# Transposes of the batch norm and the middle attention stage moved to DMAs per subtile, and SyncE's issues reordered

## The chip, the cores and the metric

The kernel runs on one core of a Trainium2 chip. The metric is the device time of one execution in microseconds (us), median of the runs shown; lower is better. Engines: PE is TensorE (matmuls), ACT is ScalarE, DVE is VectorE, POOL is GpSimd, SP is SyncE, whose queue (SPq in the profile) issues most DMAs.

## What is computed

Four graph layers over 10,000 nodes with 512 features and 5,000 edges, each followed by a residual and a layer norm. The change touches the tail of layer 1 (GraphSAGE with batch norm) and the start and middle of layer 2 (two graph attention convolutions):

```python
# layer 1, tail
h = (h - mu) * rsqrt(var + EPS) * gamma + beta
x = layernorm(x + relu(h) + x)
# layer 2, gat_conv twice; x:[n,d_in], W:[d_in,H*C], H = 4, C = 256
h = (x @ W).reshape(n, H, C)
...
out = segment_sum(h[src] * alpha[:, :, None], dst) + bias
x1 = relu(gat_conv(x, W1)); x2 = relu(gat_conv(x1, W2)); x2 @ Wfc + bfc
```

## The kernel before, in words

The program is a row of stages; at the end of each, all five engines meet at one semaphore. Nodes are padded to G = 20 groups of 512, each group being S = 4 subtiles of 128 rows. Every f32 matmul is made of three f16 ones (`split_product`, lines 324 to 326): an operand is split in a high half and the low half that is left, and lo x hi, hi x lo and hi x hi are summed in a PSUM bank. The stationary operand of a product has to have the features on the partitions, so rows (nodes on the partitions) have to be transposed first.

**`batch_norm_stage(kn, "sage")`** (lines 2037 to 2275) loads for group g the batch-norm input `b_h` (features on the partitions) and the residual rows `b_x`. ACT applies scale, shift and Relu (`apply`, L2186, 4 instructions a group). PE transposes the result to rows (`turn_rows`, L2230, 16 matmuls of 128x128 against an identity a group, f32). DVE adds the residual from PSUM (L2147), takes the norm's moments (L1607, L1610), POOL forms the power (L1616, L1619) and DVE applies it to give `b_o` (L1627). Then PE transposes `b_o` back (`turn_back`, L2240, again 16 a group, into two banks `tq`), ACT writes the high half `b_z_hi` (L2192), DVE the low half `b_z_lo` (L2161), both from PSUM, and PE multiplies each subtile with the first attention weight: 3 thirds of 344 columns, 4 chunks, 3 matmuls, so 36 a subtile and 144 a group. ACT evacuates each third to one of two buffers `b_wide` (L2207), SP stores it (L2108). POOL adds `fc_b` to `b_o` (L2123) and SP stores that (L2098). PE's list for group g is the products of g with the two kinds of transposes of group g + 1 put between them.

**`gat_middle_stage`** (lines 2282 to 2479) is between the two attention convolutions. POOL gathers the edge sums into `t_z` (L1638), SP loads the rows `h1` (L2332), DVE combines them (L2400, four a subtile) and adds a bias row (L2405), ACT writes Relu to `t_r` (L2418) and the high half to `t_row_hi` (L2421), POOL the low half to `t_row_lo` (L2374). One DMA per half and group transposes 128 x 4096 f16 values from SBUF to SBUF (L2340 the high half, L2343 the low one). PE multiplies: 72 matmuls a subtile, 288 a group, into two sets of three banks. ACT evacuates (L2432), SP stores (L2348). `sync` issues load, transposing DMAs and stores in one list; PE begins a group when both transposing DMAs of that group have landed.

The stage before these, `gin_stage`, has the same kind of DMA in the size 128 x 2048 (L1693, L1696), from a high half that ACT (L1787) and a low half that DVE (L1757) write from rows in SBUF.

In the text below "the first product" is the first matmul of L324 in a stage, and "a landing" is the moment at which a DMA's semaphore counts.

## Time and profile before

| | us |
|---|---|
| median of 3 runs | 3969.2 |
| lowest, highest | 3963.12, 3970.68 |
| the profiled execution, its own time | 3969.53 |
| its span from first to last instruction | 3967.8 |
| PE busy in the span | 3459.0 (87%) |
| DVE, ACT, POOL busy | 2125.2, 1473.6, 1466.4 |
| mean granted clock of TensorE, share of full | 0.929 |

The profile is one execution. Busy times of PE are sums over matmuls whose ends are modelled and overlap, so the rate of PE is read from the starts of neighbours, and its idle times from the waits. PEclk is the granted TensorE clock as a share of the full 2.4 GHz. A DMA's "duration" on SPq is the time for which SP was held by its issue, not its transfer.

### The profile page before, as it was taken

The page shows a single profiled execution, that of the slowest core. Times are in us where ns is not written, and L with a number is a line of the kernel's source. Part 1 is how long each engine was busy: PE and PEld are TensorE (multiplying, and loading weights), DVE is VectorE, ACT ScalarE, POOL GpSimd, SP SyncE. Part 2 cuts the span into 40 slices and gives each one's busy share as a digit, 9 for nine tenths or more (in the row PEclk, how much of TensorE's full clock was granted, in tenths as well). Part 3 has the DMA queues.
Part 4 walks back from the last instruction along what each step waited for, and adds up shares of the span by engine and source line. Part 5 has one row for each costly group of instructions (what it writes and reads, how often), then busy time and mean ns, then how long its engine had stood idle before and what let it go on. Part 6 is the DMA issues. An engine that isn't in the chain of part 4 may idle for free. (4 is left out here: it accounts for less than half of the span.)

```text
span 3967.8 us, 56467 instructions
## 1 busy us (share of the span) xinstructions
PE 3459.0 (87%) x19736; PEld 2112.9 (53%) x19736; DVE 2125.2 (54%) x3972; ACT 1473.6 (37%) x2580; POOL 1466.4 (37%) x1231
## 2 busy tenths in 40 slices
PE   4679998989979999884899999998859999859964
PEld 3134443545647777663566666665635555415543
DVE  7257775845544444376534334311748888406667
ACT  1323333533324444353333333222534444233357
POOL 2345552225322222353423323312536666334312
PEclk7789998989989999897999999999979999979976
DMA  2667774656646666496976676743966777376558
GB/s 81 199 182 204 197 196 144 205 181 227 229 155 216 215 216 217 168 279 205 214 213 193 203 211 186 206 128 103 278 239 231 262 256 262 130 239 186 176 165 275
DMA packets 533341, 800.35 MB, mean 202 GB/s; under 512 B 287494, under 2 KB 287494, under 8 KB 531152
## 3 DMA queue, kind: packets, MB, share of 16 engines
q1 hardware_dynamic: 466000, 577.37, 44.7%
q0 software_dynamic: 67200, 221.25, 19.4%
q8 instruction: 71, 1.16, 0.1%
q14 instruction: 70, 0.57, 0.0%
HBM read 470.83 MB, written 263.59 MB: 185 GB/s over the span
## 5 line engine op out<-in xcount | busy, mean ns | idle before, releaser
L325 PE MATMUL bank<-w_lo,t_r_hi 128*128 128x344 f16 (+1 forms) x2560 | 837.5, 327 | 0.0
L326 PE MATMUL bank<-w_hi,t_r_hi 128*128 128x344 f16 (+1 forms) x2560 | 837.3, 327 | 0.0
L324 PE MATMUL bank<-w_hi,w_lo 128*128 128x344 f16 (+1 forms) x1280 | 418.9, 327 | 30.8 <-DMA w_lo<-g_row_lo 30.8
L2400 DVE SCALAR_TENSOR_TENSOR t_z<-w_lo,t_z 128x256 f32<-128x256 f32 x320 | 203.9, 697 | 444.6 <-DMA w_lo<-h 442.1
L2374 POOL TENSOR_TENSOR t_row_lo<-t_r,t_row_hi 128x1024 f16<-128x1024 f32 x80 | 180.0, 2250 | 521.1 <-ACT t_row_hi L2421 521.0
L326 PEld LDWEIGHTS bank<-w_hi,t_r_hi 128*128 128x128 f16 x2560 | 250.9, 98 | 168.5 <-issue 0.6
L324 PE MATMUL bank<-w_hi 128*128 128x344 f16 x960 | 297.9, 310 | 47.3 <-DMA w_hi<-t_row_lo 46.5
L325 PEld LDWEIGHTS bank<-w_lo,t_r_hi 128*128 128x128 f16 x2560 | 250.9, 98 | 162.2 <-issue 0.5
L324 PE MATMUL bank<-w_hi,b_z_lo 128*128 128x344 f16 x960 | 297.0, 309 | 0.0
L325 PE MATMUL bank<-w_lo,b_z_hi 128*128 128x344 f16 x960 | 297.0, 309 | 0.0
L326 PE MATMUL bank<-w_hi,b_z_hi 128*128 128x344 f16 x960 | 296.9, 309 | 0.0
L2432 ACT ACTIVATE w_hi<-bank 128x344 f32<-128x344 f32 x240 | 108.9, 457 | 502.6 <-PE bank L326 496.1
L324 PE MATMUL bank<-l_z_hi,w_lo 128*128 128x512 f16 x640 | 242.8, 379 | 1.4 <-DVE l_z_lo L2783 1.4
L324 PE MATMUL bank<-w_hi,t_r_lo 128*128 128x512 f16 x640 | 243.1, 380 | 0.0
L325 PE MATMUL bank<-l_z_lo,w_hi 128*128 128x512 f16 x640 | 242.8, 379 | 0.0
L326 PE MATMUL bank<-l_z_hi,w_hi 128*128 128x512 f16 x640 | 242.7, 379 | 0.0
L2576 POOL TENSOR_TENSOR t_r_lo<-t_r,t_r_hi 128x512 f16<-128x512 f32 x160 | 196.2, 1234 | 96.8 <-ACT t_r_hi L2644 90.2
L2641 ACT ACTIVATE t_r<-bank,vec_scaled 128x512 f32<-128x512 f32 x160 | 109.7, 685 | 292.6 <-PE bank L2672 240.9
L2207 ACT ACTIVATE b_wide<-bank 128x344 f32<-128x344 f32 x240 | 108.5, 455 | 279.5 <-PE bank L326 242.5
L1638 POOL DMA_INDIRECT t_z<-sum_gat,slot_i x160 | 165.2, 1032 | 122.6 <-SPq L291 79.8
L1616 POOL TENSOR_TENSOR n_power<-n_moments,eps 128x4 f32<-128x4 f32 x80 | 16.0, 200 | 506.8 <-DVE n_moments L1610 506.8
L2607 DVE SCALAR_TENSOR_TENSOR t_z<-w_lo,t_z 128x256 f32<-128x256 f32 x320 | 186.8, 643 | 21.5 <-DMA t_z<-sum_gat,slot_i 13.1
(353 smaller groups left out, 7307.1 us busy)
## 6 DMA issues: line engine op xcount, KB each, us to landing
w_lo<-h SPq DMA_DIRECT2D x160, 512.0 KB
h<-b_wide SPq DMA_DIRECT2D x80, 516.0 KB, 2.7
h<-w_hi SPq DMA_DIRECT2D x80, 516.0 KB, 3.2
sum_gat<-a_out SPq DMA_DIRECT2D x80, 514.0 KB
l_x<-x SPq DMA_DIRECT2D x40, 1024.0 KB
sum<-e_out SPq DMA_DIRECT2D x120, 256.0 KB
g_x<-in_x SPq DMA_DIRECT2D x20, 1024.0 KB
x<-g_y SPq DMA_DIRECT2D x20, 1024.0 KB
```

The lines of the kernel that those rows point to most:

```text
L324: pe.matmul(out, s_lo, m_hi, start=(k == 0), stop=False)
L325: pe.matmul(out, s_hi, m_lo, start=False, stop=False)
L326: mm = pe.matmul(out, s_hi, m_hi, start=False, stop=last)
L1616: self.nc.gpsimd.tensor_tensor(self.power[:, u, :], self.moments[:, u, :, 1], self.kn.eps[:], ALU.add)\
L1638: pool.indirect_dma_start(out, None, sums, bass.IndirectOffsetOnAxis(ap=kn.slot_i[:, g * S + s:g * S + s + 1], axis=0), bounds_check=kn.d. ...
L2207: act.activation(wide[s % 2][:, n * THIRD:(n + 1) * THIRD], mm[n], ACT.Copy, scale=UNSCALE)\
L2374: nc.gpsimd.tensor_tensor(row_lo[:, s, :], r_f[s % 2][:], row_hi[:, s, :], ALU.subtract)\
L2400: ins = v.scalar_tensor_tensor(out=z[u][:, s, cols], in0=hrow[:, s, cols], scalar=z[u][:, s, HC + h:HC + h + 1], in1=z[u][:, s, cols], op0 ...
L2432: act.activation(wide[s % 2][:, third * THIRD:(third + 1) * THIRD], mm[s % 2][third], ACT.Copy, scale=UNSCALE).then_inc(wide_done.sem, 1)
L2576: g_.tensor_tensor(r_lo[:, u, k, :], r_f[k % 2][:], r_hi[:, u, k, :], ALU.subtract)\
L2607: ins = v.scalar_tensor_tensor(out=z[u][:, s, cols], in0=hrow[:, s, cols], scalar=z[u][:, s, HC + h:HC + h + 1], in1=z[u][:, s, cols], op0 ...
L2641: act.activation(r_f[k % 2][:], tp[k % 4][:], ACT.Relu, scale=A_SCALE, bias=kn.vec_scaled[:, bias + k:bias + k + 1]).then_inc(r_done.sem, 1)
```

## The change

It does three things. In the batch norm stage it drops `turn_back`: ACT and DVE write the two halves from `b_o` as rows in SBUF (`b_row_hi`, `b_row_lo`), and eight DMAs a group (two halves, four subtiles, 128 x 512 each) transpose them into dead weight space. In the middle stage the two DMAs a group become eight (128 x 1024 each), and semaphores count landings per subtile, so that PE, ACT and POOL wait for a subtile and no longer for a group. In both stages SP's list is written out in another order; in the batch norm stage loads go out two groups further ahead, `b_wide` has four buffers, and the list is no loop any more. PE's `turn_rows` is done for two groups ahead of the first product, then for group g + 2 after subtile 0 of group g.

```diff
@@ batch_norm_stage @@
-        z_hi = kn.buffer(mem, "b_z_hi", [P, 2, 4, D], F16)
-        z_lo = kn.buffer(mem, "b_z_lo", [P, 2, 4, D], F16)
-        wide = two("b_wide", [P, GAT_ROW], F32)
+        row_hi = kn.buffer(mem, "b_row_hi", [P, S, D], F16)
+        row_lo = kn.buffer(mem, "b_row_lo", [P, S, D], F16)
...
+        wide = [kn.buffer(mem, f"b_wide{s}", [P, GAT_ROW], F32) for s in range(S)]
...
-    tp = [[kn.bank[n] for n in (0, 1, 0, 1)]] * 2 if sage else [kn.bank[0:4], kn.bank[4:8]]
-    tq = [kn.bank[2], kn.bank[3]]
+    tp = [kn.bank[0:4]] * 2 if sage else [kn.bank[0:4], kn.bank[4:8]]
...
+        def turn(g, s):
+            u = g % 2
+            if g >= 2:
+                sp.wait_ge(prod.sem, prod.at((g - 1) * S * THIRDS))
+            sp.wait_ge(turned_in[s].sem, turned_in[s].at(g * 32))
+            for rows, done, out in ((row_hi, hi_done, z_hi), (row_lo, lo_done, z_lo)):
+                sp.wait_ge(done.sem, done.at(g * S + s + 1))
+                sp.dma_start(out[u][:, s * 4:(s + 1) * 4, :], rows[:, s, :], transpose=True)\
+                    .then_inc(turned_in[s].sem, 16)
...
+            for s in range(S):
+                turn(0, s)
+            store(0, 0)
+            for g in range(G):
+                if g + 1 < G:
+                    for s in range(S):
+                        turn(g + 1, s)
+                store_wide(g, 0)
+                if g + 4 < G:
+                    load_h(*divmod(g + 4, 2))
+                if g + 1 < G:
+                    store(*divmod(g + 1, 2))
+                store_wide(g, 1)
+                if g + 4 < G:
+                    load_x(*divmod(g + 4, 2))
+                store_wide(g, 2)
+                store_wide(g, 3)
...
         def low_parts(i, u):
-            for k in range(4):
-                dve.wait_ge(hi_done.sem, hi_done.at(g * 4 + k + 1))
-                v.scalar_tensor_tensor(out=z_lo[:, u, k, :], in0=tq[k % 2][:], scalar=A_SCALE, in1=z_hi[:, u, k, :],
+            for s in range(S):
+                dve.wait_ge(hi_done.sem, hi_done.at(g * S + s + 1))
+                dve.wait_ge(turned_in[s].sem, turned_in[s].at(g * 32))
+                v.scalar_tensor_tensor(out=row_lo[:, s, :], in0=o[u][:, s, :], scalar=A_SCALE, in1=row_hi[:, s, :],
...
+                if s == 1 and ahead(i, G) and (u == 0 or ahead(i + 1, G)):
+                    apply(*following(i + 1, u))
+                if s == 3 and ahead(i, G):
+                    high_parts(i + 1, u)
...
         def group(i, u, last):
...
             products(i, u, 0)
-            if not last:
-                turn_rows(*following(i, u), (2, 3))
-            products(i, u, 1)
-            products(i, u, 2, (0, 1))
-            if not last:
-                turn_back(*following(i, u), (0, 1))
...
+            if ahead(i, G):
+                turn_rows(i + 1, u, range(S))
+            for s in range(1, S):
+                products(i, u, s)
@@ gat_middle_stage @@
-    turned_in = pair("turned_in", 32 * H)
+    turned_in = kn.sig.several(S, "turned_in", 32 * G)
...
+        for s in range(S):
+            load_rows(0, s)
+        for s in range(S):
+            load_rows(1, s)
+            turn(0, s)
+        for s in range(S):
+            load_rows(2, s)
         for g in range(G):
-            if g + 1 < G:
-                turn(g + 1)
-            store_wide(g, 0)
-            if g + 3 < G:
-                load_rows(g + 3)
-            for s in range(1, S):
+            for s in range(S):
+                if g + 1 < G:
+                    turn(g + 1, s)
+                if g + 3 < G:
+                    load_rows(g + 3, s)
                 store_wide(g, s)
...
@@ tensor @@
-            pe.wait_ge(turned_in[u].sem, turned_in[u].at(i * 32 + 32))
             for s in range(S):
+                pe.wait_ge(turned_in[s].sem, turned_in[s].at(g * 32 + 32))
```

SP's list at the start of the batch norm stage, as far as the first products need it. The number behind `b_h`, `b_x` is the buffer (115 and 117 even groups, 116 and 118 odd ones); L2090 is `load_h`, L2095 `load_x`, L2104 `turn`. Before:

```order
L2087 DMA b_h_115<-h 128x4x512 [waits stored1,stored0,meet,rows_turned0]
L2091 DMA b_x_117<-x 128x4x512 [waits y_done_0]
L2087 DMA b_h_116<-h 128x4x512 [waits rows_turned1]
L2091 DMA b_x_118<-x 128x4x512 [waits y_done_1]
L134 UNCONDITIONAL_BRANCH
L134 ISA
L2087 ISA [waits rows_turned0]
L2087 DMA b_h_115<-h 128x4x512
```

Of the change:

```order
L2090 DMA b_h_116<-h 128x4x512 [waits rows_turned1]
L2095 DMA b_x_118<-x 128x4x512 [waits y_done_1]
L2090 DMA b_h_115<-h 128x4x512 [waits rows_turned0]
L2095 DMA b_x_117<-x 128x4x512 [waits y_done_0]
L2090 DMA b_h_116<-h 128x4x512 [waits rows_turned1]
L2095 DMA b_x_118<-x 128x4x512 [waits y_done_1]
L2104 DMA_TRANSPOSE w_hi<-b_row_hi 128x4x128 [waits hi_done,turned_in0]
L2104 DMA_TRANSPOSE w_lo<-b_row_lo 128x4x128 [waits lo_done]
L2104 DMA_TRANSPOSE w_hi<-b_row_hi 128x4x128 [waits hi_done,turned_in1]
```

The first transposing DMA stands behind the load of `b_x` for group 3, which waits until DVE has read `b_x` of group 1.

SP's list at the start of the middle stage. `w_lo<-h` is `load_rows`, `t_row_hi` and `t_row_lo` are the sources of the transposing DMAs. Before:

```order
L2332 DMA w_lo<-h 128x1024 x3
L2332 DMA w_lo<-h 128x1024 [waits z_mixed] x4
L2340 DMA_TRANSPOSE t_r_hi_178<-t_row_hi 128x32x128 [waits hi_done]
L2343 DMA_TRANSPOSE w_hi<-t_row_lo 128x32x128 [waits lo_done]
L2332 DMA w_lo<-h 128x1024 [waits z_mixed] x4
```

Of the change:

```order
L2347 DMA w_lo<-h 128x1024 x3
L2347 DMA w_lo<-h 128x1024 [waits z_mixed]
L2357 DMA_TRANSPOSE t_r_hi_180<-t_row_hi 128x8x128 [waits hi_done,turned_in0]
L2357 DMA_TRANSPOSE w_hi<-t_row_lo 128x8x128 [waits lo_done]
L2347 DMA w_lo<-h 128x1024 [waits z_mixed]
L2357 DMA_TRANSPOSE t_r_hi_180<-t_row_hi 128x8x128 [waits hi_done,turned_in1]
L2357 DMA_TRANSPOSE w_hi<-t_row_lo 128x8x128 [waits lo_done]
```

The loads of group 1 and the transposing DMAs of group 0 now alternate, a subtile at a time.

## Rows read from the trace of the kernel before

**Rows 1.** Busy time by stretch: us, busy and count per engine, PEclk, DMA share, GB/s.

```profile
1166.00:1651.00 485.00, 484.46 (x3473) 348.82 (x3471) 199.16 (x376) 199.62 (x388) 109.12 (x57) 1.00 0.57 203
1894.00:2702.00 808.00, 807.14 (x5516) 540.63 (x5517) 277.91 (x360) 252.23 (x380) 239.82 (x144) 1.00 0.68 190
```

**Rows 2.** Timeline of PE inside the batch norm stage: start, us, instruction.

```profile
1232.89 0.31 PE L326 MATMUL bank<-w_hi,b_z_hi 128*128 128x344 f16 x1
1233.04 1.04 PE L2240 MATMUL bank<-ident,b_o 128*128 128x128 f32 x8
1233.91 0.31 PE L324 MATMUL bank<-w_hi,b_z_lo 128*128 128x344 f16 x1
```

**Rows 3.** Timeline of PE, first and last product of the batch norm stage.

```profile
1164.02 0.49 PE L324 MATMUL bank<-w_hi,b_z_lo 128*128 128x344 f16 x1
...
1650.15 0.31 PE L326 MATMUL bank<-w_hi,b_z_hi 128*128 128x344 f16 x1
```

**Rows 4.** Timeline of PE, first products of the middle stage.

```profile
1894.10 0.47 PE L324 MATMUL bank<-w_hi 128*128 128x344 f16 x1 [46.51 <-DMA w_hi<-t_row_lo]
...
1899.23 0.43 PE L324 MATMUL bank<-w_hi 128*128 128x344 f16 x1
1899.49 0.31 PE L325 MATMUL bank<-w_lo,t_r_hi 128*128 128x344 f16 x1
1899.64 0.31 PE L326 MATMUL bank<-w_hi,t_r_hi 128*128 128x344 f16 x1
```

**Rows 5.** Timeline of DVE, group 0 of the batch norm stage.

```profile
1149.31 0.66 DVE L2147 SCALAR_TENSOR_TENSOR b_y<-b_x,bank 128x512 f32<-128x512 f32 x1
...
1150.94 0.65 DVE L2147 SCALAR_TENSOR_TENSOR b_y<-b_x,bank 128x512 f32<-128x512 f32 x1
...
1154.20 1.91 DVE L1627 TENSOR_SCALAR b_o<-b_y,n_moments,n_power 128x512 f32<-128x512 f32 x4 [1.54 <-POOL n_power L1619]
```

**Rows 6.** By tile, gin stage: ns min/median/max, first and last start, forms.

```profile
L1787 ACT ACTIVATE g_row_hi<-g_z x80: 624/630/631, 212.0 to 620.4; 128x512 f16<-128x512 f32 x80
L1757 DVE SCALAR_TENSOR_TENSOR g_row_lo<-g_z,g_row_hi x80: 684/693/693, 212.7 to 621.1; 128x512 f16<-128x512 f32 x80
L1693 SPq DMA_TRANSPOSE w_hi<-g_row_hi x20: 1575/2194/3201, 218.7 to 621.1; - x20
L1696 SPq DMA_TRANSPOSE w_lo<-g_row_lo x20: 1660/2366/3857, 220.7 to 623.1; - x20
DMA to landing us min/median/max: 4.4/4.6/5.5
```

**Rows 7.** Timeline of SP in the middle stage, its start and one later group.

```profile
1868.95 4.93 SPq L2340 DMA_TRANSPOSE t_r_hi<-t_row_hi  x1
1873.93 17.96 SPq L2343 DMA_TRANSPOSE w_hi<-t_row_lo  x1
...
2241.83 4.99 SPq L2343 DMA_TRANSPOSE w_lo<-t_row_lo  x1
2246.87 0.58 SPq L2348 DMA_DIRECT2D h<-w_hi  x1
```

**Rows 8.** Timeline of ACT and POOL, group 0 of the middle stage.

```profile
1855.68 1.05 ACT L2421 CAST t_row_hi<-t_r 128x1024 f16<-128x1024 f32 x1
1856.81 2.47 POOL L2374 TENSOR_TENSOR t_row_lo<-t_r,t_row_hi 128x1024 f16<-128x1024 f32 x1 [3.15 <-ACT t_row_hi L2421]
1871.50 1.01 POOL L1638 DMA_INDIRECT t_z<-sum_gat,slot_i  x1 [0.15 <-issue]
```

**Rows 9.** Busy time by stretch, columns as in rows 1.

```profile
1239.20:1263.70 24.50, 24.50 (x178) 17.72 (x177) 10.62 (x21) 10.31 (x20) 5.74 (x3) 1.00 0.61 215
1856.00:1860.00 4.00, 0.00 (x0) 0.00 (x0) 3.96 (x5) 2.82 (x3) 2.88 (x2) 0.50 1.02 393
1860.00:1864.00 4.00, 0.00 (x0) 0.00 (x0) 3.96 (x4) 0.10 (x1) 1.93 (x1) 0.50 0.76 280
1880.00:1884.00 4.00, 0.00 (x0) 0.00 (x0) 1.78 (x3) 0.00 (x0) 0.00 (x0) 0.50 1.21 113
```

More of the change, by code:

```diff
@@ L128, in settle, with in_pairs @@
     eng.sem_inc(kn.passed, 1)
-def in_pairs(eng, n, body):
-    if n > 2:
-        with eng.Fori(0, n // 2 - 1) as i:
+def in_pairs(eng, n, body, apart=1):
+    if n > 2 * apart:
+        with eng.Fori(0, n // 2 - apart) as i:
             for u in range(2):
                 body(i, u, False)
-    body(n // 2 - 1, 0, False)
-    body(n // 2 - 1, 1, True)
+    for i in range(n // 2 - apart, n // 2):
+        body(i, 0, False)
+        body(i, 1, i == n // 2 - 1)
 def ahead(i, n):
@@ L2126, in group @@
         def group(i, u, last):
[L2127 to L2129 removed]
+            norm.pool(pool, i, u)
+            bias(i, u)
         if sage:
[L2132 to L2133 removed]
             in_pairs(pool, G, group)
@@ L2174, in group_alone @@
             finish(i, u)
-        residual(0, 0, range(S))
         if sage:
-            finish(0, 0)
-            low_parts(0, 0)
-        in_pairs(dve, G, group if sage else group_alone)
+            in_pairs(dve, G, group)
+        else:
+            residual(0, 0, range(S))
+            in_pairs(dve, G, group_alone)
     def scalar(act):
@@ L2213, in scalar @@
             high_parts(0, 0)
-            in_pairs(act, G, group)
+            apply(1, 0)
+            high_parts(0, 1)
+            in_pairs(act, G, group, 2)
         else:
@@ L2231, in turn_rows, with products @@
                 ins.then_inc(rows_turned[u].sem, 1)
-        def turn_back(i, u, chunks=range(4)):
+        def products(i, u, s):
             g = i * 2 + u
-            pe.wait_ge(rows_out[u].sem, rows_out[u].at(i * S + S))
-            for k in chunks:
-                pe.wait_ge(lo_done.sem, lo_done.at(g * 4 + (k - 1 if k >= 2 else 0)))
-                for s in range(S):
-                    ins = pe.transpose(tq[k % 2][:, s * P:(s + 1) * P], o[u][:, s, k * P:(k + 1) * P], kn.ident[:])
-                ins.then_inc(turned[u].sem, 1)
-        def products(i, u, s, thirds=range(THIRDS)):
-            g = i * 2 + u
-            parts = lambda k: (z_hi[:, u, k, s * P:(s + 1) * P], z_lo[:, u, k, s * P:(s + 1) * P])
-            for n in thirds:
+            parts = lambda k: (z_hi[u][:, s * 4 + k, :], z_lo[u][:, s * 4 + k, :])
+            pe.wait_ge(turned_in[s].sem, turned_in[s].at(g * 32 + 32))
+            for n in range(THIRDS):
                 pe.wait_ge(wide_done.sem, wide_done.at((g * S + s - 1) * THIRDS + n + 1))
@@ L2253, in group @@
         def group(i, u, last):
-            pe.wait_ge(lo_done.sem, lo_done.at((i * 2 + u) * 4 + 4))
-            if not last:
-                turn_rows(*following(i, u), (0, 1))
             products(i, u, 0)
-            if not last:
-                turn_rows(*following(i, u), (2, 3))
-            products(i, u, 1)
-            products(i, u, 2, (0, 1))
-            if not last:
-                turn_back(*following(i, u), (0, 1))
-            products(i, u, 2, (2,))
-            products(i, u, 3, (0,))
-            if not last:
-                turn_back(*following(i, u), (2, 3))
-            products(i, u, 3, (1, 2))
+            if ahead(i, G):
+                turn_rows(i + 1, u, range(S))
+            for s in range(1, S):
+                products(i, u, s)
         if sage:
             turn_rows(0, 0, range(S))
-            turn_back(0, 0)
+            turn_rows(0, 1, range(S))
             in_pairs(pe, G, group)
@@ L2326, in sync, with load_rows, turn @@
     def sync(sp):
[L2327 to L2336 removed]
+        def load_rows(g, s):
+            if g:
+                sp.wait_ge(z_mixed.sem, z_mixed.at((g - 1) * S + s + 1))
+            sp.dma_start(hrow[:, s, :], dram["h1"][g * GROUP + s * P:g * GROUP + (s + 1) * P, LOGITS:])\
+                .then_inc(h_in[s].sem, 16)
+        def turn(g, s):
+            u = g % 2
             if g >= 2:
                 sp.wait_ge(prod.sem, prod.at((g - 1) * S * THIRDS))
[L2339 to L2344 removed]
+            sp.wait_ge(turned_in[s].sem, turned_in[s].at(g * 32))
+            for rows, done, out in ((row_hi, hi_done, r_hi), (row_lo, lo_done, r_lo)):
+                sp.wait_ge(done.sem, done.at(g * S + s + 1))
+                sp.dma_start(out[u][:, s * CH:(s + 1) * CH, :], rows[:, s, :], transpose=True)\
+                    .then_inc(turned_in[s].sem, 16)
         def store_wide(g, s):
```

107 lines of the change are left out of this document (44 added, 63 removed).

## The prediction

> **What bounds the kernel now.** I read the busy time by stretch first. From 1166 us to the end of the batch norm stage PE is busy 484.46 of 485 us at the full clock, and in the middle stage 807.14 of 808 us, while DVE, ACT and POOL have work for less than half of it and the DMA share is 0.57 and 0.68 [rows 1]. So in both stages only two things can be won: instructions that PE no longer issues, and an earlier first product. The timeline of PE gives the prices at full clock. From the start of one product to what follows it is 0.146 us (1232.89 to 1233.04), and eight of the transposes take 0.87 us (1233.04 to 1233.91), so 0.109 us each [rows 2]. A group of the batch norm stage before is 144 x 0.146 + 32 x 0.109 = 24.5 us. Check over the stage: 2880 products and the 600 transposes that follow the first product make 420.5 + 65.4 = 485.9 us; measured is 1164.02 to 1650.15 plus one step, 486.3 us [rows 3]. PE has no hole there.
>
> The other thing to see is a cold start. The middle stage's PE waits 46.51 us in one piece for the transposed low half and then issues 18 products up to 1899.23, 5.1 us, so 0.285 us each, where the full clock would have 0.146: the half clock (1.2 GHz) costs 2.5 us there [rows 4].
>
> **Batch norm stage, PE's work.** `turn_back` goes: 20 x 16 = 320 transposes, of which 16 stood before the first product. Two groups of `turn_rows` are done before the first product instead of one and a half. After the first product there remain 18 x 16 = 288 transposes, 31.4 us, in place of 65.4 us: a gain of 34 us. A group takes 21.0 + 1.75 = 22.8 us.
>
> **Batch norm stage, its start.** Here the new order of SP costs. The first transposing DMA stands behind the load of `b_x` of group 3, and that waits until DVE has read `b_x` of group 1. DVE's list is: residual and moments of group 0, apply, low halves of group 0, then the residual of group 1. Before, the apply starts at 1154.20 and takes 1.91 us, so it ends at 1156.1; one subtile of residual and moments is 1150.94 - 1149.31 = 1.63 us [rows 5]. High and low halves from rows in SBUF are those of the stage with the same form: 0.630 us on ACT, 0.693 us on DVE [rows 6]. Low halves: 4 x 0.69 to about 1158.9. The fourth residual of group 1 ends 3 x 1.63 + 0.65 later, 1164.5. Then SP issues the load (0.5 us), then the first high and low halves. A DMA of four times that size lands 4.4 to 5.5 us after its issue with SP held for 2.2 us of it [rows 6]; the quarter needs some 0.6 + 2.3 us, and 1 MB of `b_x` is before it in the queue, 2.6 us at 393 GB/s [rows 9]. I take the first product at 1170.2, with 1168 (nothing waits for the load) and 1173 (the whole 4.4 us, behind the load) as ends: 6.2 us later than 1164.02. PE has been idle then since its last transposes near 1153, so it starts at the half clock as in rows 4: 2.5 us, of which about 0.4 us (486.3 - 485.9) was paid before too. The stage's last product ends at 1170.2 + 420.5 + 31.4 + 2.5 = 1624.6 instead of 1650.3: **25.7 us earlier** (23 to 28).
>
> **What has to stay hidden in a group of 22.8 us.** ACT has 12 evacuations, four applies and four high halves, in all much what it had (10.31 us of 24.5 [rows 9]); a high half costs 0.03 us more. DVE keeps its 10.62 us, POOL its 5.74. SP: eight transposing DMAs, each between 0.58 us (a plain store's hold [rows 7]) and 2.2 us (the hold of one four times as large [rows 6]), so 4.6 to 17.6 us, plus at most 7 x 0.58 = 4.1 us for the rest: it fits even at the upper end, and I take 1 us each, nearest to a quarter of 2.2 us plus the fixed part. They are issued at the start of group g for group g + 1, so they have 22.8 us; the tightest reader is ACT's high half of g + 2 after subtile 2's products, about 17 us on, which must find the row buffer read out. The DMA engines: 0.61 x 24.5 = 14.9 us of work a group before [rows 9], plus 2 x 0.52 MB of transposes. The middle stage's low half is 1.05 MB too and holds SP 4.99 us in a steady group [rows 7]; beside POOL's gathers the same DMA held it 17.96 us. The batch norm stage has no gathers, so I take 5 us: 19.9 of 22.8 us, cost nothing. At 18 us it would be 32.9 us and the DMAs would set the pace (first rival).
>
> By the Trainium skill ("DMA: Bandwidth & Descriptors", the rule on batching), DMAs should be batched to 1 MiB for three quarters of peak, each having a fixed cost of about 2 us; the change goes to 128 and 256 KiB. The trace has a high half still landing (4.4 us) when the low half's issue begins after 2.2 us [rows 6], so such DMAs overlap. By that fixed cost paid one after another the eight would take 16 us more and the DMA work 36 us a group (rival 2's mechanism); by the rows it is hidden.
>
> **Middle stage, its start.** PE's work is unchanged; only the first product moves, now 1894.10, with the half clock on either side. The high half of subtile 0 is there at 1855.68 + 1.05 = 1856.7, the low one at 1856.81 + 2.47 = 1859.3 [rows 8]. Before, SP issued only at 1868.95, after all four subtiles, and the low half crawled beside the gathers that POOL started at 1871.50 (17.96 us; the DMA share is above 1 at only 113 GB/s there) [rows 7, 8, 9]. After, subtile 0's two DMAs are issued at 1856.8 and 1859.4, when the DMA engines are still full (393 GB/s) and then free up (280 GB/s, 0.76) [rows 9]. A quarter of the crawling time is 4.5 us each, a quarter of the undisturbed one 1.25 us: the low half lands between 1859.4 + 1.25 + 2 and 1856.8 + 9 + 2, so 1863 to 1868. I take 1867, near the slow end since the gathers of two groups are in flight. The other subtiles land about 3 to 5 us apart, and PE needs one every 10.5 us. **27 us earlier** (18 to 31). One thing may take some back: ACT still prepares all of group 1 before its first evacuation. PE's six banks last until 1867 + 2.5 + 144 x 0.146 = 1890.5; ACT's last cast waits for POOL's low half after the gathers issued from 1871.50 on, which I get at 1884 to 1888. It just fits.
>
> In steady groups SP's transposing DMAs now sit between stores, so subtile 3 of g + 1 goes out after the store of subtile 2, 32 us into a group of 42; PE needs it 31 us into the next one. That costs nothing; ACT may wait a little longer for the row buffer, and an evacuation has 21 us before its bank is wanted.
>
> **Sum.** -25.7 - 27 = -52.7 us. The profiled execution's 3969.53 is 0.3 us above the median 3969.2 and its parts outside the span do not change, so 3969.2 - 52.7 = 3916.5, **3917 us**.
>
> **Rivals.**
> 1. *The DMA engines become the bound of the batch norm stage and the kernel gets slower.* Mechanism: transposes share the engines with 1 MB loads and the stores, and crawl as they do beside gathers: 14.9 + 18 = 32.9 us a group, 658 us for 20, against 486: +172, +6 for the start, -27: 4120 us. It decides from 22.8 - 14.9 = 7.9 us of transposing a group; above 10.7 us the whole kernel is slower than before. For it: rows 7's 17.96 us and the 113 GB/s. Against it: the queue is SP's alone here, and in steady middle groups with stores and loads around it it is 4.99 us. Chance 0.03. The same half way, at 9.6 us: a group keeps its 24.5 us, the start costs 8: 3969 + 8 - 27 = 3950. Chance 0.05.
> 2. *Small transposing DMAs do not overlap.* Each of the eight waits for the one before to land, 4.4 us [rows 6]: 35 us a group, 704 us, +218 - 27: 4160 us. Against it the overlap of two in rows 6, though those are larger. Chance 0.015. The Trainium skill ("VectorE: DVE Perf Modes", the three transpose paths) gives 390 ns for a 128x128 block on TensorE and 1309 ns by DMA and says to use TensorE where PSUM will do. By that a group's 32 blocks would take 41.9 us, worse than this rival; the trace has 0.109 us on PE and 32 blocks in 2.19 + 2.37 us of SP's hold [rows 6].
> 3. *The middle's early start is given back.* Subtile 0 waits behind the gathers, or ACT's first evacuation comes after 1890.5 and PE stalls: 10 to 18 us of the 27 are left: 3926 to 3934. For it: the gathers' 18 us crawl, ACT's fit with 2 to 6 us. Chance 0.13.
> 4. *The batch norm's start does not change* (the load of group 3 is no obstacle), so 8 us more: 3909. Chance 0.04. That the start of either stage gains nothing because loads, not the order, set it, is excluded for the middle by the 46.5 us that PE waits on the low half's DMA alone.
>
> **How the numbers follow.** The forecast (3911 to 3924) has 0.735, rival 3 0.13, rival 4 0.04, half-way DMA bound 0.05, the slow ones 0.045. The range goes to 3906 (rival 4 with a middle start at 1863) and to 3938 (rival 3 with a batch norm start at 1173), leaving out the DMA-bound cases, 0.095. A measurement of this kernel tells about 0.2%, 8 us, from nothing. Faster by more: 0.95; within: 0.005; slower: 0.045.
>
> **What would show it.** PE busy time without L2240 and 288 transposes after the first product; groups of 22.8 us; the first product of the batch norm stage about 1170 with SP having waited on `b_y` of group 1; DMA share near 0.88 in the stage; the middle's wait of PE for its first transposed half down from 46.5 to about 20 us, and no wait of PE on L2432's successor above a microsecond. The prediction is wrong if PE waits on `row_lo` DMAs within groups, if a 128x512 transposing DMA holds SP for over 2.2 us, or if PE stalls after the sixth bank of the middle stage.

## The result, and the profile after

| us | before | after |
|---|---|---|
| median of the comparison | 3969.94 (3963.12 to 3972.34, 4 runs) | 3913.07 (3912.64 to 3921.49, 4 runs) |
| ratio, 95% interval | | 0.9865 [0.9846, 0.9883] |
| span of the profiled execution | 3967.8 | 3911.1 |
| PE busy, instructions | 3459.0, x19736 | 3419.3, x19416 |
| q1 (SP's queue), share of 16 engines' span | 44.7% | 50.3% |

The kernel is faster by 56.9 us; 3917 with 3906 to 3938 was forecast. To see where the time left, I cut each profiled span at points that every version has: SP's first load of a stage, its first product and its last product. All numbers are differences of starts in the timelines of SP and PE. The table compares one profiled execution of each kernel. How far two executions can differ shows in its first stretch, which has no edit: it took 1136.54 us here and 1141.51 in the second profile of the kernel before (c_before), and 1135.6 to 1142.5 over all fourteen profiles.

| us | before | after | change |
|---|---|---|---|
| start to batch norm's first load | 1136.54 | 1136.86 | +0.3 |
| to its first product | 27.48 | 34.03 | +6.6 |
| first to last product | 486.13 | 452.79 | -33.3 |
| to the middle stage's first load (no edit there) | 192.55 | 189.25 | -3.3 |
| to its first product | 51.40 | 24.09 | -27.3 |
| first to last product | 843.41 | 847.38 | +4.0 |
| rest (no edit there) | 1230.29 | 1226.70 | -3.6 |

The timeline of PE in the kernel after: the first product of batch norm, with the half clock at its start, and the 16 transposes of `b_h` that are left in a group. These answer to [rows 2, 3].

```profile
1170.89 0.47 PE L325 MATMUL bank<-w_hi,w_lo 128*128 128x344 f16 x1 [16.99 <-DMA w_lo<-b_row_lo]
...
1245.88 1.91 PE L2266 MATMUL bank<-ident,b_h 128*128 128x128 f32 x16
...
1314.12 1.91 PE L2266 MATMUL bank<-ident,b_h 128*128 128x128 f32 x16
```

From 1245.88 to 1314.12 are three groups, 22.75 us each. The products have 0.287 us steps for the first 11 (to 1173.99, half clock) and 0.146 behind them. The windows view of the kernel after: a group and a long stretch of batch norm (answering to [rows 9]), the middle stage's start, and its steady part.

```profile
core 0: us, PE busy (x) PEld busy (x) DVE busy (x) ACT busy (x) POOL busy (x), PEclk, DMA share, GB/s
1245.88:1268.62 22.74, 22.74 (x162) 15.86 (x160) 10.32 (x20) 10.26 (x20) 5.73 (x3) 1.00 0.94 289
1400.00:1500.00 100.00, 100.00 (x708) 70.14 (x706) 44.46 (x86) 45.90 (x89) 25.93 (x13) 1.00 0.96 291
1837.00:1880.00 43.00, 41.46 (x264) 26.75 (x264) 37.55 (x46) 15.34 (x19) 24.24 (x15) 0.93 1.10 272
2006.00:2600.00 594.00, 594.00 (x4076) 398.36 (x4074) 231.01 (x265) 182.21 (x283) 176.03 (x109) 1.00 0.82 193
```

PE has no hole in batch norm, but the DMA share went from 0.61 to 0.94. The view by tile gives SP's hold of one transposing DMA (minimum, median, maximum in ns) of `b_row_hi` and `b_row_lo`, with the landing of the low halves, and then the hold for the middle stage's `t_row_lo`:

```profile
L2104 SPq DMA_TRANSPOSE w_hi<-b_row_hi x80: 1188/1206/4033, 1164.7 to 1592.0; - x80
L2104 SPq DMA_TRANSPOSE w_lo<-b_row_lo x80: 1258/1268/5316, 1166.0 to 1593.2; - x80
DMA to landing us min/median/max: 2.5/2.6/9.6
...
L2357 SPq DMA_TRANSPOSE w_hi<-t_row_lo x40: 1262/1673/6767, 1830.4 to 2592.7; - x40
L2357 SPq DMA_TRANSPOSE w_lo<-t_row_lo x40: 1315/1570/6959, 1862.6 to 2634.7; - x40
```

What SP does in one group of batch norm after, from its timeline, and what it waits for from 1400 to 1500 (the waits view):

```profile
1400.98 1.68 SPq L2104 DMA_TRANSPOSE w_hi<-b_row_hi  x1
1402.70 3.81 SPq L2104 DMA_TRANSPOSE w_lo<-b_row_lo  x1
1406.62 2.03 SPq L2104 DMA_TRANSPOSE w_hi<-b_row_hi  x1
1408.69 1.65 SPq L2104 DMA_TRANSPOSE w_lo<-b_row_lo  x1
...
1419.27 0.81 SPq L2122 DMA_DIRECT2D h<-b_wide  x1
1423.28 0.33 SPq L2122 DMA_DIRECT2D h<-b_wide  x1
1423.72 1.36 SPq L2104 DMA_TRANSPOSE w_hi<-b_row_hi  x1
...
SPq L2122 <- ACT b_wide L2243: 18.5, 7, 4.1
SPq L2104 <- PE bank L327: 7.4, 10, 1.0
```

From 1400.98 to 1423.72, one whole group, SP waits once: from 1420.08 to 1423.28, 3.2 us, until ACT has filled `b_wide`. Its other rows follow each other with 0.1 us or less between them; so 19.5 of 22.7 us are issuing. The waits view has 18.5 us of waits for ACT in the 100 us (4.4 groups). The 7.4 us that it puts down to PE lie inside holds of transposing DMAs and can't be waits: in SP's list `store_wide(g - 1, 3)` stands ahead of `turn(g + 1, s)`, and that store already needs all products of group g - 1, which is what `turn` would wait for. Two resources, DMA share and SP, thus stand near their ends, and PE still sets the pace. Which of the two is next is the question of runs e4, e6 and e8.

The middle stage's first product in the kernel after, and the waits of PE from 1820 to 1960; they answer to [rows 4]:

```profile
1837.02 0.47 PE L325 MATMUL bank<-w_hi 128*128 128x344 f16 x1 [19.19 <-DMA w_hi<-t_row_lo]
1862.61 0.32 PE L325 MATMUL bank<-w_hi 128*128 128x344 f16 x1 [1.52 <-ACT w_hi L2447]
...
PE bank L325 <- DMA w_hi<-t_row_lo: 19.2, 1, 19.2
PE bank L325 <- ACT w_hi L2447: 4.1, 3, 1.5
```

The wait for the low half fell from 46.5 to 19.2 us, and a new one, for ACT to empty a bank, takes 4.1 us: the 4.0 us by which the products take longer. The wait of 1.52 us stands at product 144, the first that needs a seventh bank. ACT's and SP's timelines show what it hangs on:

```profile
1861.16 1.04 ACT L2436 CAST t_row_hi<-t_r 128x1024 f16<-128x1024 f32 x1 [2.86 <-DMA w_hi<-t_row_lo]
1862.11 1.14 ACT L2447 ACTIVATE w_hi<-bank 128x344 f32<-128x344 f32 x3
...
1844.97 5.49 SPq L2357 DMA_TRANSPOSE w_hi<-t_row_lo  x1
```

The cast is ACT's last one for group 1, and the first evacuation of the stage stands behind it. It overwrites the row buffer of subtile 3, so it has to wait until group 0's transposing DMA of that buffer, issued at 1844.97, has landed, 16.2 us later.

### The profile page after: what moved, and what is told of

The parts are those of the page before. It is cut to its first block and busy times, and to the rows that moved or that the text cites. A ratio compares the mean times of both kernels' runs of the same rounds, so it can differ in the third digit from the quotient of the medians.

```text
span 3911.1 us, 55988 instructions
## 1 busy us (share of the span) xinstructions
PE 3419.3 (87%) x19416; PEld 2074.1 (53%) x19416; DVE 2155.2 (55%) x3972; ACT 1463.1 (37%) x2580; POOL 1452.1 (37%) x1231
## 3 DMA queue, kind: packets, MB, share of 16 engines
q1 hardware_dynamic: 556880, 598.37, 50.3%
## 5 line engine op out<-in xcount | busy, mean ns | idle before, releaser
L325 PE MATMUL bank<-w_hi,w_lo 128*128 128x344 f16 (+1 forms) x2240 | 716.7, 320 | 49.8 <-DMA w_lo<-g_row_lo 31.3
L2415 DVE SCALAR_TENSOR_TENSOR t_z<-w_lo,t_z 128x256 f32<-128x256 f32 x320 | 243.5, 819 | 396.4 <-DMA w_lo<-h 393.4
L326 PE MATMUL bank<-w_lo,w_hi 128*128 128x344 f16 (+1 forms) x1280 | 419.6, 328 | 0.0
L327 PE MATMUL bank<-w_hi 128*128 128x344 f16 (+1 forms) x1280 | 419.4, 328 | 0.0
L325 PE MATMUL bank<-w_hi 128*128 128x344 f16 x960 | 298.3, 311 | 21.8 <-DMA w_hi<-t_row_lo 19.2
L325 PEld LDWEIGHTS bank<-w_hi,w_lo 128*128 128x128 f16 x2240 | 219.3, 98 | 181.7 <-issue 50.8
L2622 DVE SCALAR_TENSOR_TENSOR t_z<-w_lo,t_z 128x256 f32<-128x256 f32 x320 | 187.0, 645 | 21.4 <-DMA t_z<-sum_gat,slot_i 13.3
```

The source lines that it names most:

```text
L325: pe.matmul(out, s_lo, m_hi, start=(k == 0), stop=False)
L326: pe.matmul(out, s_hi, m_lo, start=False, stop=False)
L327: mm = pe.matmul(out, s_hi, m_hi, start=False, stop=last)
L2415: ins = v.scalar_tensor_tensor(out=z[u][:, s, cols], in0=hrow[:, s, cols], scalar=z[u][:, s, HC + h:HC + h + 1], in1=z[u][:, s, cols], op0 ...
L2622: ins = v.scalar_tensor_tensor(out=z[u][:, s, cols], in0=hrow[:, s, cols], scalar=z[u][:, s, HC + h:HC + h + 1], in1=z[u][:, s, cols], op0 ...
```

## The experiments

My theory: batch norm gains by 288 transposes less on PE and pays with a later start that the load of `b_x` group 3 causes; the middle stage gains by its start, since the splitting lets PE begin with subtile 0. Rivals were a DMA-bound batch norm stage, and a middle stage that gives its start back.

**One half of the change each.** e1 has the old middle stage, e2 the old batch norm stage.

```diff
 # e1_bn_only
-def gat_middle_stage(kn): ...   (the changed one)
+def gat_middle_stage(kn): ...   (the one of the kernel before)
 # e2_mid_only: the same with batch_norm_stage
```

> Batch norm stage as changed, middle attention stage as before. If the gains are what the two stages' PE timelines say, and add up: the first product of the batch norm stage at about 1171 us, its last at 1623.5, 26 us below the kernel before, so about 3943.5 us, and the middle stage's PE waiting 46 us again for its first transposed low half. If instead the 7 us by which the whole kernel gained more than its two stages (56.9 against 26.5 + 23.3) belong to the batch norm change, by the attention stage behind it starting on quieter queues, the kernel stands near 3937.

> Middle stage as changed, batch norm stage as before. By the PE timelines: first product 27 us earlier after the stage's start (24 us behind SP's first load, 51 before), 4 us given back in three waits of PE for ACT's evacuations within the first two groups, so 23 us below the kernel before: about 3946.5 us. If the surplus of 7 us belongs to this change, about 3940.

Measured: e1 3939.61 (3933.31 to 3941.09, 4 runs), ratio 0.9922 [0.9905, 0.9939]; e2 3940.04 (3939.72 to 3940.88), 0.9929 [0.9912, 0.9946]; before 3966.94. The gains of 27.3 and 26.9 us add up to 54.2, against 56.9 for the whole: within the spread of the runs, the halves are independent. e1 came out between the two values of its expectation (3943.5 and 3937), e2 at its lower one (3940); in e2 PE waited only about 1.5 us for ACT, so little was given back. From batch norm's first load to its last product e1 takes 488.0 us and the kernel after 486.8, before 513.6. In the middle stage e2 takes 866.9 us from first load to last product, the kernel after 871.5, before 894.8.

**Batch norm's start.** The load of `b_x` of group 3 is moved behind the first turns.

```diff
-            for g in range(2, 4):
-                load_h(1, g - 2)
-                load_x(1, g - 2)
+            load_h(1, 0)
+            load_x(1, 0)
+            load_h(1, 1)
             for s in range(S):
                 turn(0, s)
+            load_x(1, 1)
             store(0, 0)
```

> The changed kernel with one load moved: b_x of group 3 goes out behind the four subtiles' transposing DMAs of group 0. If the wait of that load is what holds the first product at 1170.9 us: the first high half is issued at 1155.7, the first low half at 1157.0 to 1158, it lands 2.6 us later and the first product starts at about 1160, 10 us earlier; PE's work behind it is the same, so 9 to 10 us below the changed kernel, about 3903.5, unless PE then waits in group 0 for the rows of group 2 (its b_y of group 1 is only read at 1165). If the load is no obstacle and the DMA engines' backlog sets the start, nothing changes (3913).

Measured: 3906.25 (3902.29 to 3910.97, 4 runs), 0.984 [0.9823, 0.9856]. Timelines of PE and SP in e3 (stage's first load at 1138.29):

```profile
1157.37 1.32 SPq L2104 DMA_TRANSPOSE w_hi<-b_row_hi  x1
1158.73 1.35 SPq L2104 DMA_TRANSPOSE w_lo<-b_row_lo  x1
...
1168.94 0.57 SPq L2095 DMA_DIRECT2D b_x<-x  x1
...
1164.81 0.46 PE L325 MATMUL bank<-w_hi,w_lo 128*128 128x344 f16 x1 [9.42 <-DMA w_lo<-b_row_lo]
```

The first product stands 26.5 us behind the load instead of 34.0. So the load was the obstacle, for 7.5 us. I had expected 10: the first high half was issued at 1157.37, as forecast from the stage's first load on, but the low half behind it, issued at 1158.73, landed 5.9 us later, not 2.6. The moved load lands later and nothing waits for it: 453.1 us from first to last product, as after.

**Size and number of the DMAs.** e4 takes all four subtiles of a group in one transposing DMA for the high and one for the low half.

```diff
-                sp.wait_ge(done.sem, done.at(g * S + s + 1))
-                sp.dma_start(out[u][:, s * 4:(s + 1) * 4, :], rows[:, s, :], transpose=True)\
-                    .then_inc(turned_in[s].sem, 16)
+                sp.wait_ge(done.sem, done.at(g * S + S))
+                sp.dma_start(out[u], rows[:].rearrange("p s c -> p (s c)"), transpose=True)\
+                    .then_inc(turned_in[0].sem, 16)
```

> The changed kernel with two transposing DMAs a group in the batch norm stage (128x2048 each) in place of eight, and counts per group. If small DMAs cost nothing that is not hidden, PE's groups stay at 22.75 us and only the start moves: the first product comes after the whole group has landed, issues 1164.7 to about 1169.5 and 2.5 us to land, so about 1172, 1 us later, and the kernel stays within 2 us of 3913. If eight small ones load the DMA engines more than two large ones (a fixed price per DMA), the DMA share of the stage falls clearly below 0.95, and SP's hold a group falls from 14 us to about 5 to 7 us.

Measured: 3915.02 (3912.23 to 3924.02, 4 runs), 0.987 [0.9852, 0.9889]; no difference from the change that a measurement can tell. The windows and the tile view of e4:

```profile
1400.00:1500.00 100.00, 100.00 (x704) 69.52 (x703) 44.06 (x84) 45.55 (x90) 27.45 (x13) 1.00 0.90 275
...
L2106 SPq DMA_TRANSPOSE w_hi<-b_row_hi x20: 3041/3252/5326, 1165.1 to 1588.0; - x20
```

The hold of SP falls from four times 1.21 us to 3.25 for the high halves (medians), but the first product comes 3.7 us later (37.73 against 34.03 us after the first load), since it waits for four subtiles.

**Is the stage near the DMA engines' bound, or SP's?** e6 issues each of the change's transposing DMAs a second time, into unread space; e8 does that with e4's two. Both add 1 MB a group.

```diff
 # e6_bn_twice (counts doubled to 64 a group); e8_batched_twice the same with e4's form
+            for rows, done, out in ((row_hi, hi_done, again[0]), (row_lo, lo_done, again[1])):
+                sp.dma_start(out[u][:, s * 4:(s + 1) * 4, :], rows[:, s, :], transpose=True)\
+                    .then_inc(turned_in[s].sem, 16)
```

> The change, with each transposing DMA of the batch norm stage issued twice, the second copy into space that nothing reads (1 MB more a group). It prices the DMA work of the transposes and tells how near the stage is to being bound by DMA. In the kernel before the DMA engines were busy 0.61 of a group of 24.5 us, 14.9 us; in the changed kernel 0.96 of 22.74 us, 21.8 us: 6.9 us of DMA work a group for the transposes, if that share is work. Theory A (the share is work, the stage now stands just under the bound of the DMA engines): the doubled kernel needs 21.8 + 6.9 = 28.7 us a group, TensorE waits about 6 us a group, 20 groups give +120 us, the kernel comes to about 4030. Theory B (much of the share is packets that wait for each other while the engines have room): groups stay between 22.7 and 24.5 us, the kernel between 3913 and 3950. A third bound is SyncE's own issue: eight more holds of about 1.2 us on top of about 20 us of stores, loads and turns a group, which would also lead to groups of 28 to 30 us, but with the DMA share well under 0.9; the share tells it from theory A.

> The run e4_bn_batched with each of its two transposing DMAs of a group issued twice, the second copy unread: the same extra megabyte a group as e6_bn_twice, in two more DMAs instead of eight. In e6_bn_twice a group took 32.1 us at a DMA share of 0.80; SyncE's queue was busy with issuing for about 27 of them (22.7 less 5.9 us of waits in the changed kernel, 16.8, and eight holds of 1.27 us more), and ScalarE waited for the transposes before its next preparation. Theory A (issue on SyncE and the waits queued behind it made the 32 us): here the issue grows by about 5.5 us to about 14 us a group, TensorE keeps its 22.7 us, or loses a few tenths, and the kernel comes out between 3912 and 3935. Theory B (the DMA engines cannot carry the extra megabyte in 22.7 us, whatever the share says): groups take 26 us or more, the kernel 3980 or more. At 32 us, as in e6_bn_twice, SyncE would be cleared.

Measured: e6 4109.71 (4104.51 to 4114.64, 4 runs), 1.0356 [1.0339, 1.0374]; e8 3958.2 (3952.91 to 3975.46, 10 runs), 0.998 [0.9969, 0.9991]. From first to last product e6 takes 641.4 us, 32.1 a group, and e8 486.2, 24.3 a group. The windows view, of e6 and below the dots of e8:

```profile
1300.00:1500.00 200.00, 151.50 (x964) 100.08 (x962) 63.88 (x120) 62.15 (x120) 34.34 (x18) 0.85 0.80 222
...
1300.00:1500.00 200.00, 187.89 (x1275) 127.97 (x1274) 83.13 (x160) 81.06 (x160) 45.48 (x25) 0.97 1.07 294
```

The same bytes, and e6 moves them at 222 GB/s with a share of 0.80 where e8 has 294 GB/s; the packets' time of a group is the same (0.80 x 32.1 = 25.7 us, 1.07 x 24.3 = 26.0). So the DMA engines are not what makes a group of e6 32 us. SP's timeline in e6 goes from one first store of a group to the next, with sixteen holds between:

```profile
1410.99 0.58 SPq L2127 DMA_DIRECT2D h<-b_wide  x1
...
1416.02 4.67 SPq L2106 DMA_TRANSPOSE w_hi<-b_row_hi  x1
1420.73 4.33 SPq L2106 DMA_TRANSPOSE w_lo<-b_row_lo  x1
1425.11 1.71 SPq L2109 DMA_TRANSPOSE w_hi<-b_row_hi  x1
...
1443.90 0.58 SPq L2127 DMA_DIRECT2D h<-b_wide  x1
```

It is 32.9 us, and SP waits nowhere in it: all its rows follow each other with about 0.1 us or less between them. Sixteen transposing DMAs hold it for 27.0 us, the seven others for 4.6. In e6 SP's issuing is what sets the pace. The first holds, behind the group's loads and stores, are far longer than the median of 1.2 to 1.27 us, which is why the 28 to 30 us a group of the third bound (and the 27 us of issuing in the expectation of e8) were too little. The waits view of e6 (1300 to 1500) shows how the other engines come to wait:

```profile
ACT b_row_hi L2234 <- DMA w_lo<-b_row_lo: 60.3, 17, 4.9
PE bank L325 <- ACT b_wide L2248: 48.5, 6, 8.8
```

SP issues late, ACT waits for the row buffer to be read out, its evacuations queue behind that wait, PE waits for a bank. Of the 9.3 us that eight more DMAs cost a group, two larger ones with the same bytes cost 1.6, between theory A (a few tenths) and theory B (3 us or more). In e8 SP has almost no gap either, but in another way:

```profile
1324.04 11.35 SPq L2108 DMA_TRANSPOSE w_hi<-b_row_hi  x1
1335.44 2.70 SPq L2108 DMA_TRANSPOSE w_lo<-b_row_lo  x1
```

The DMA that held SP for 3.25 us in e4 holds it for 11.35 us here, behind the stores and loads of the group and with a DMA share of 1.07. That points to the DMA queue itself as the bound of e8, at 294 GB/s, and the changed kernel's 291 GB/s in the window above is not far from it. No run shows it: PE also waits 12.1 us for ACT in e8's stretch, and ACT 28.1 us for the low halves.

**Splitting or order in the middle stage.** e5 keeps the DMAs per subtile but puts SP's list in its old order.

```diff
-        for s in range(S):
-            load_rows(1, s)
-            turn(0, s)
+        for s in range(S):
+            load_rows(1, s)
+        for s in range(S):
+            turn(0, s)
...
+            if g + 1 < G:
+                for s in range(S):
+                    turn(g + 1, s)
+            store_wide(g, 0)
```

> The change, except that SyncE's list in the middle stage stands in its old order: the four loads of group 1 ahead of the first transposing DMA, the four turns of group g+1 together ahead of the first store of group g, the loads of group g+3 together behind that store. The DMAs stay per subtile with their own counts. The changed kernel has its first product of the stage 24.1 us after SyncE's first load, the kernel before 51.4 us. Theory A (the splitting does most of it, since TensorE can begin with subtile 0): the first transposing DMA goes out behind the last load of group 1 and the first product stands 28 to 32 us after the first load; the kernel comes out 4 to 8 us behind the changed kernel, near 3920. Theory B (the order does most of it): the first product stands 42 to 50 us after the first load and the kernel is 18 to 25 us behind, near 3935. If the order matters within the groups too, TensorE shows waits for turned subtiles in the steady part (between 2006 and 2600 us), where the changed kernel shows none; both theories expect none.

Measured: 3919.75 (3914.81 to 3927.3, 4 runs), 0.9879 [0.986, 0.9898]. SP's and PE's timelines, and the steady part:

```profile
1815.52 24.27 SPq L2347 DMA_DIRECT2D w_lo<-h  x8
1839.90 1.28 SPq L2357 DMA_TRANSPOSE t_r_hi<-t_row_hi  x1
...
1846.00 0.46 PE L325 MATMUL bank<-w_hi 128*128 128x344 f16 x1 [25.58 <-DMA w_hi<-t_row_lo]
...
2006.00:2600.00 594.00, 594.00 (x4075) 398.56 (x4074) 218.33 (x266) 190.64 (x283) 190.68 (x109) 1.00 0.68 192
```

The first product stands 30.5 us behind the load, as theory A had it: the splitting gives 20.9 of the 27.3 us, the order 6.4. In these profiles the order's 6.4 are lost at once: e5 has no wait of PE for ACT, its products take 841.6 us, and from first load to last product it needs 872.0 us, where the kernel after needs 871.5. The order does raise the DMA share of the steady part, 0.82 instead of 0.68 at nearly the same GB/s (193 and 192), while PE is busy throughout in both.

**The wait for ACT.** e7 is e3 with one preparation of group 1 behind the first three evacuations.

```diff
-            for s in range(S):
+            for s in range(S if u == 0 else 3):
                 parts(0, u, s)
...
+                if isinstance(i, int) and g == 0 and n == 2:
+                    parts(0, 1, 3)
```

> The run e3_x_behind, and in the middle stage ScalarE's preparation of subtile 3 of group 1 stands behind its first three evacuations, not ahead of them. In e3_x_behind TensorE waited 9.4 us in the first groups of that stage for ScalarE to empty a bank, in the changed kernel 4.1 us. Theory A (the wait comes from ScalarE standing in its last preparations when the first products are done): the wait goes to 1 us or less, and the products of the stage take 843.5 to 845 us from first to last instead of 847 to 854; the kernel comes to 3898 to 3905. Theory B (ScalarE is held by late operands, and what moved behind only moves the wait to the product of group 1 that needs subtile 3): TensorE waits 4 to 9 us for turned subtile 3 of group 1 near 40 us after its first product, and the time stays at 3906.

Measured: 3911.74 (3908.09 to 3916.56, 4 runs), 0.9858 [0.9841, 0.9874]: no gain over e3. The wait moved. PE's and ACT's timelines of e7:

```profile
1865.55 0.32 PE L325 MATMUL bank<-w_hi 128*128 128x344 f16 x1 [0.90 <-ACT w_hi L2448]
1874.98 0.32 PE L325 MATMUL bank<-w_hi 128*128 128x344 f16 x1 [2.26 <-ACT w_hi L2448]
...
1873.53 1.04 ACT L2437 CAST t_row_hi<-t_r 128x1024 f16<-128x1024 f32 x1 [6.74 <-DMA w_lo<-t_row_lo]
1874.48 0.80 ACT L2448 ACTIVATE w_hi<-bank 128x344 f32<-128x344 f32 x2
```

ACT's cast for group 2 waits for group 1's low half, and the evacuation stands behind it. Neither theory had this right: the wait at the seventh bank that A meant is gone (0.8 us in e3, product 144), but it was the small one; the large one, 8.3 us at product 216 in e3, hangs on the casts for group 2. B foresaw that the wait only moves and the time stays, but put it at the landing of subtile 3, where no wait is.

**Repeats, a control, and a last combination.** c_before is the kernel before, r_after the change, r_x_behind e3 once more; e9 joins e3's batch norm with e5's middle stage.

> The kernel before, unchanged, profiled once more. In the profiles of the kernels above, stretches that no edit touches differ: from the last product of batch norm to the first load of the middle stage 192.6 us (before), 189.3, 187.9, 190.7; from the last product of the middle stage to the end 1230.3, 1226.7, 1225.4, 1229.6. Theory A (run to run variation): this profile has them anywhere in 187 to 193 and 1223 to 1231. Theory B (the change shortens them by shifting the loads behind it): it has them at 192.6 and 1230.3 within 0.5.

> The changed kernel, unchanged, beside its variants on the same chip: 3912 to 3917. From the stage's first load to its last product the middle stage took 871.5 us in its first profile and 866.9 and 872.0 us in two kernels with the same middle stage; a value of 866 to 873 is expected here, with 1.5 to 5 us of TensorE waiting for ScalarE. The stretches that no edit touches: 187 to 191 and 1223 to 1228 if the lower values belong to the program, up to 193 and 1231.5 if they vary from run to run (the kernel before had 192.6 and 1230.3, then 192.8 and 1231.5).

> The kernel of e3_x_behind once more, beside the changed kernel: if its lead is the 7.5 us of its earlier first product in batch norm, it stands 4 to 10 us under r_after; if in the middle stage the 8.3 us wait of TensorE for ScalarE was chance, that wait is 1 to 5 us here and the middle stage takes 867 to 873 us from first load to last product, where it took 877.

> The list of e3_x_behind in batch norm together with the middle stage's list of e5_mid_old_order: the first product of batch norm 7.5 us earlier than in the changed kernel, and in the middle stage a start 6 us later but with no wait of TensorE for ScalarE (e5_mid_old_order: 872.0 us from the stage's first load to its last product, the changed kernel 871.5, e2_mid_only 866.9, e7_act_late 869.4). Expected: 6 to 9 us under the changed kernel, 3904 to 3909. If what e3_x_behind won in batch norm was chance, it comes out within 3 us of the changed kernel.

Measured: c_before 3971.19 (3965.73 to 3974.83, 8 runs), ratio 0.9999 [0.9989, 1.001]; r_after 3912.68 (3909.61 to 3921.64, 4 runs), 0.9856 [0.9841, 0.9871]; r_x_behind 3904.59 (3904.01 to 3906.19, 5 runs), 0.984 [0.9827, 0.9853]; e9 3909.26 (3906.81 to 3912.02, 5 runs), 0.9848 [0.9835, 0.9862]. r_x_behind is 8.1 us below r_after, as its start 7.9 us earlier (26.25 against 34.13) has it. It is the best version here: one load moved in SP's list. r_after had its median where it was expected, but its profiled execution, the slowest of its four, waited 12.1 us for ACT, not 1.5 to 5. e9 missed its expectation: it is 3.4 us below r_after, not 6 to 9, and 4.7 us above r_x_behind.

The profile of r_after shows rival 3 at its largest. Timelines of SP, ACT and PE:

```profile
1864.87 6.57 SPq L2357 DMA_TRANSPOSE w_lo<-t_row_lo  x1
...
1866.12 1.06 ACT L2433 ACTIVATE t_r<-t_z 128x1024 f32<-128x1024 f32 x1 [4.07 <-issue]
1881.25 1.04 ACT L2436 CAST t_row_hi<-t_r 128x1024 f16<-128x1024 f32 x1 [14.07 <-DMA w_lo<-t_row_lo]
1882.20 0.80 ACT L2447 ACTIVATE w_hi<-bank 128x344 f32<-128x344 f32 x2
...
1882.70 0.47 PE L325 MATMUL bank<-w_hi 128*128 128x344 f16 x1 [10.62 <-ACT w_hi L2447]
```

The low half of group 1's first subtile is issued at 1864.87 beside loads and gathers, ACT gets its row buffer back 16 us later, and the evacuation right behind the cast is what PE waits for, 10.6 us. The kernels with the changed middle stage, by PE's wait for ACT near its start and the time from first load to last product:

| | e2 | e6 | after | e4, r_x_behind | e8 | e3 | r_after |
|---|---|---|---|---|---|---|---|
| wait, us | 1.5 | 3.4 | 4.1 | 4.5 | 5.1 | 9.4 | 12.1 |
| load to last product | 866.9 | 868.9 | 871.5 | 872.0, 871.7 | 870.8 | 877.1 | 878.9 |

The second row follows the first. The old order has 872.0 and 874.4 (e5, e9): within the spread of the new one, whose mean is 872.2. But r_after and e3 were profiled in their slowest executions, and the whole times say more: each of the five runs of e9 is slower than each of the five of r_x_behind (3906.81 to 3912.02 against 3904.01 to 3906.19), which differs from it in this order alone; and e5 gains 51.4 us on the kernel before (3971.12 beside it) where the change gains 56.9 and 56.1. So the order of SP's list in the middle stage earns some 5 us of the time, though the single profiles do not show where.

## Why the prediction was right

- **PE's work in batch norm.** 31.4 + 420.5 us plus the half clock were forecast from first to last product, 454.4; measured 452.8. A group: 22.8 forecast, 22.74 measured.
- **Its start.** First product forecast at 1170.2, measured 1170.89, and e3 shows the reason right: 7.5 us hang on the load. The half clock lasted 3.1 us and cost about 1.5, not 5.1 and 2.5 as I took over from rows 4; that is this execution's, for in r_after it lasted 5.1 us at the same place, and first to last product took 453.8.
- **SP's hold.** 1 us taken, 1.2 measured as the median, with longer ones behind a group's loads and stores. The sign I had set for being wrong, a hold over 2.2 us, did appear (3.81 us above), without effect: SP had 3.2 us a group of waits to spare.
- **DMA share.** 0.88 forecast, 0.94 and 0.96 measured. I had read the share as work against a capacity of 1. e8 shows 1.07 while PE is busy 94% of the time, and the middle stage 1.10, so a share is not work against a capacity of 1, and the step "19.9 of 22.8 us, cost nothing" came out right on wrong grounds. With small DMAs the next bound is SP: I had called its 4.6 to 17.6 us, plus 4.1, a fit; it issues for 19.5 of 22.7 us, and eight more DMAs cost 9.3 us a group, with SP never idle.
- **The rule on batching** of the Trainium skill ("DMA: Bandwidth & Descriptors", section "Bandwidth") asks for fewer and larger DMAs. In this stage e4 goes half the way, to 512 KiB, and gains nothing; e8 against e6 (24.3 against 32.1 us a group) shows it decide once the issuing queue has no slack. The Trainium skill's 1309 ns for a 128x128 block by DMA ("VectorE: DVE Perf Modes", section "The three transpose paths") is twice what a 128x512 piece shows, where four blocks landed 2.6 us after issue (median), 0.65 us a block, with others beside it.
- **The middle's start.** Forecast 27 us earlier, measured 27.3, and 19.2 us of wait for "about 20". The splitting alone, with the list in its old order, gives 20.9 of them (e5).
- **"It just fits"** was the step that failed, in a small size. The stage's first load is at 1842.70 before and at 1812.93 after, so the forecast, which is in the times of the kernel before, is to be read 29.8 us earlier: ACT's last cast of group 1 at 1854 to 1858, PE's six banks used up at 1860.7. The banks lasted until 1861.1, as forecast. The cast came at 1861.16, because I had counted POOL's low half ahead of it but not the transposing DMA of group 0 that has to read the row buffer out first (2.86 us of wait, a landing of 16.2 us beside the gathers). So PE did stall after the sixth bank, 1.5 us, which was the third sign of being wrong. The casts for group 2, each ahead of an evacuation and each waiting for such a DMA, I had not counted at all; they cost the other 2.6 us. That is rival 3's mechanism in a small size; it takes 1.5 to 12.1 us back, 4.1 in the profile after.
- **The sum.** -26.8 + 0.3 for batch norm and -23.3 for the middle make 49.8 us of the profiled 56.7; 52.7 was forecast. The remaining 6.9 us lie in stretches without an edit, which the forecast had at nothing. Without them the kernel would stand near 3920, still in the range and about as far from 3917 as it is now, on the other side.

The cause of those 6.9 us stays open. I took them for variation, and the control speaks against it: c_before has 192.8 and 1231.5 us in the two stretches, no less than before. They lie in the same code twice, the start of the stage that follows each of the two stages. Its first matmul of L1576 (L1577 where the lines have moved by one) comes 178.8 and 179.9 us after the last product of batch norm and of the middle stage in the profile before, 179.1 and 178.3 in c_before, and 174.0 to 177.7 in the twelve profiles of changed kernels, e1 and e2 among them, whichever half is changed. Behind that matmul the kernel before takes 1050.4 us to its end and the one after 1051.0. No run here tells how an edit elsewhere shortens that code.

## What to carry to other kernels

Here, moving transposes from a bound TensorE to DMAs paid their full TensorE time, because the issuing queue had room. Look at the waits that are left on that queue's engine (3.2 of 22.7 us) rather than at the DMA share, and take its holds from a timeline: the medians (1.2 us for 128x512, 1.6 for 128x1024) leave out the long ones behind loads and stores. In an in-order list, look at what stands behind each wait: one load ahead of the first transposes cost 7.5 us, and a cast that waits for its buffer ahead of an evacuation up to 10.6 us. An earlier start is worth only what the next engine in the ring can follow; here the waits for ACT took 1.5 to 12.1 us of it back. And a single profiled execution can be the slow one: compare medians before calling a gain nothing.

## What the runs showed of the hardware

- The DMA share of a window goes past 1 (1.10 at 272 GB/s, 1.07 at 294 GB/s) and falls when the same DMAs are issued in another order (0.82 and 0.68 at 193 and 192 GB/s), with PE busy throughout. The pair repeats between 2006 and 2600 us: 0.80 to 0.86 in r_after, r_x_behind, e2, e3 and e4, 0.68 in e9, which has the old order. So the share alone is no distance to a bound.
- A transposing DMA holds SP for 1.2 us with 128x512, and 3.25 us (high half) or 1.98 (low half) with 128x2048, by the medians: less than in proportion. But the hold depends on what is queued: 1.20 to 4.67 us for the same 128x512 in one group of e6, 3.25 us in e4 and 11.35 in e8 for the same 128x2048.
- The half clock (1.2 GHz) at the two cold starts lasted 3.1 and 6.0 us, though PE had been idle for 17.0 and 19.2 us, much alike; in r_after, the same program, it lasted 5.1 and 6.0 us after 18.3 and 17.5 us.
- A transposing DMA of 128x1024 in the middle stage landed 3.7 us after its issue as the median and 16.3 at most, the latter beside the gathers.
